# The multiply of the slot sums, on GpSimd instead of VectorE, in a graph kernel on one core

## The reference, cut to what matters

```python
h = x @ gcn_w                                      # one column
deg = segment_sum(ones, dst)                       # edges and loops
dis = rsqrt(deg)
msg = h[src] * (dis[src] * dis[dst])[:, None]
spa = sigmoid(segment_sum(msg, dst) + gcn_b)
return x * spa + x + chn_se                        # chn_se: the channel gate
```

## Time and profile before

| what | us |
|---|---|
| median of three runs | 8827.48 |
| lowest and highest run | 8819.26, 8833.81 |
| the profiled execution | 8835.66 |
| its span in the profile | 8833.9 |
| the loop, first one-hot (3441.20) to the first copy behind it (3668.73) | 227.5 |

### The profile page before, as it was taken

The page is one execution under the profiler, slowest core; times in us unless marked ns, Lnnn a source line. Parts: engine busy times, 40 slices in busy tenths (PEclk is TensorE's granted clock), DMA queues, the critical chain, the costliest instruction groups (busy, mean ns, idle before and its releaser), DMA issues. The chain is left out here.

```text
span 8833.9 us, 128810 instructions
## 1 busy us (share of the span) xinstructions
PE 5536.4 (63%) x23276; PEld 3811.3 (43%) x23277; DVE 4591.1 (52%) x13076; ACT 1797.8 (20%) x3217; POOL 4384.5 (50%) x4493
## 2 busy tenths in 40 slices
PE   5566666688888878976666666795444444444443
PEld 4333333455666556744444444453333333333332
DVE  8766666545555557854444444464333333333334
ACT  4000000046666631122222222341000000000000
POOL 0466666536666660034444444104666666666664
PEclk7566666699999987687877787896555555555555
DMA  2233333332222222322222222311111113111112
GB/s 78 58 100 105 102 105 103 94 113 82 82 84 80 83 66 62 128 87 65 65 65 63 67 67 64 75 32 44 53 52 44 44 44 43 43 43 43 44 43 60
DMA packets 310617, 612.39 MB, mean 69 GB/s; under 512 B 90042, under 2 KB 164102, under 8 KB 310344
## 3 DMA queue, kind: packets, MB, share of 16 engines
q0 software_dynamic: 185408, 469.86, 20.3%
q1 hardware_dynamic: 125064, 141.13, 5.3%
HBM read 566.94 MB, written 50.13 MB: 70 GB/s over the span
## 5 line engine op out<-in xcount | busy, mean ns | idle before, releaser
L834 PE MATMUL bank<-ring,oh 128*128 128x128 f32 x3552 | 1164.7, 475 | 1558.9 <-issue 838.8
L834 PEld LDWEIGHTS bank<-ring,oh 128*128 128x128 f32 x3552 | 861.8, 309 | 1861.8 <-issue 1150.4
L601 POOL DMA_INDIRECT ring<-q_table,stage_i x888 | 841.3, 947 | 1067.7 <-DVE ring L2181 693.9
L601 POOL DMA_INDIRECT ring<-h_table,stage_i x888 | 881.2, 992 | 641.9 <-issue 326.3
L1791 DVE TENSOR_TENSOR acc<-bank,acc 128x256 f32 x1776 | 753.6, 424 | 771.6 <-PE bank L907 386.3
L601 POOL DMA_INDIRECT ring<-fwd_table,stage_i x888 | 839.9, 946 | 578.1 <-issue 308.9
L601 POOL DMA_INDIRECT ring<-bwd_table,stage_i x888 | 840.1, 946 | 513.5 <-issue 272.8
L1826 DVE TENSOR_TENSOR acc<-bank,acc 128x128 f32 x1776 | 518.5, 292 | 1040.3 <-issue 689.2
L1252 ACT ACTIVATE ring<-big 128x889 f16<-128x889 f16 x840 | 832.4, 1033 | 514.4 <-PE bank L918 383.4
L918 PE MATMUL bank<-ring,big 128*128 128x445 f16 (+1 forms) x3360 | 819.0, 367 | 137.1 <-ACT ring L1252 108.5
L627 POOL DMA_INDIRECT big<-x_and_degree,stage_i x536 | 537.2, 1002 | 397.4 <-PE bank L867 225.9
(11 more groups left out here) (425 smaller groups left out, 7574.1 us busy)
## 6 DMA issues: line engine op xcount, KB each, us to landing
big<-places_in_block SPq DMA_DIRECT2D x111, 256.0 KB
acc<-places_in_block SPq DMA_DIRECT2D x74, 384.0 KB
ring<-h_table,stage_i POOLq DMA_INDIRECT x888
ring<-q_table,stage_i POOLq DMA_INDIRECT x888
ring<-fwd_table,stage_i POOLq DMA_INDIRECT x888
ring<-bwd_table,stage_i POOLq DMA_INDIRECT x888
big<-x_and_degree,stage_i POOLq DMA_INDIRECT x536
h_table<-hq SPq DMA_DIRECT2D x50, 128.0 KB, 1.7
```

The source lines that it names most:

```text
L601: pool.indirect_dma_start(out=gbuf[:, u % RING, 0:width], out_offset=None, in_=table, in_offset=bass.IndirectOffsetOnAxis(ap=stage_i[:, v, ...
L834: pe.matmul(bank[u % 4][:, 0:width], oh[:, u % 4, :], gbuf[:, u, 0:width], start=True, stop=True).then_inc(S["mm"], 1)
```

## The change

The 74 multiplies move from VectorE's queue to GpSimd's, ahead of its wait for `spa_in`, with the same operands and the same two waits. GpSimd runs them in order of the batches. VectorE's loop keeps the three one-hots of `select_slots`. A new semaphore, `slot_low`, is given by the low digits' one-hot, and PE waits for it in `slot_sums` beside `slot_prod`, because the two operands now come from two engines.

```diff
+            def place_values(b, k):        # in GpSimd's program
+                pool.wait_ge(S["slot_cp"], b + 1 + 3)
+                pool.wait_ge(S["slot_eq"], b + 1)
+                pool.tensor_tensor(high_val[k].rearrange("p u (s n r) -> p u s n r", s=3, r=2),
+                                   high_eq[k].rearrange("p u (n r) -> p u n r", r=2).unsqueeze(2).to_broadcast([P, BATCH, 3, NP // 2, 2]),
+                                   val_pairs[k].unsqueeze(3).to_broadcast([P, BATCH, 3, NP // 2, 2]), ALU.mult).then_inc(S["slot_prod"], 1)
+            for b in range(2):
+                place_values(b, b)
+            with pool.Fori(0, BATCHES // 3) as i:
+                for k in range(3):
+                    place_values(i * 3 + 2 + k, (2 + k) % 3)
...
             def slot_sums(b, k):
                 pe.wait_ge(S["slot_prod"], b + 1 + 3)
+                pe.wait_ge(S["slot_low"], b + 1)
...
-                dve.tensor_tensor(by_pairs(low_oh[k], P), iota_pairs(P), over(dst_lo[:, t, :], P), ALU.is_equal)
-
-            def place_values(b, k):
-                dve.wait_ge(S["slot_cp"], b + 1 + 3)
-                dve.wait_ge(S["slot_eq"], b + 1)
-                o = dve.tensor_tensor(...)
-                o.then_inc(S["slot_prod"], 1)
+                dve.tensor_tensor(by_pairs(low_oh[k], P), iota_pairs(P), over(dst_lo[:, t, :], P), ALU.is_equal).then_inc(S["slot_low"], 1)
...
                 select_slots(1, 1, 0)
-                place_values(0, 0)
                 with dve.Fori(0, BATCHES // 3) as i:
                     for k in range(3):
                         select_slots(i * 3 + 2 + k, (2 + k) % 3, i + (2 + k) // 3)
-                        place_values(i * 3 + 1 + k, (1 + k) % 3)
-                place_values(BATCHES - 1, 1)
```

More of the change, by code:

```diff
@@ L302, in build @@
         d_t d_at d_m d_h d_m2 d_h7 d_res x_in wb_in consts_in col_ready col_done gate_step
-        gate_done spa_in spa_out pass_ready p_split l2_oh l2_t l2_cp l2_p l2_add l2_silu
+        gate_done spa_in spa_out pass_ready slot_low p_split l2_oh l2_t l2_cp l2_p l2_add l2_silu
         l2_c l2_acc sqrt_in sqrt_out x2_done x2_mul x2_stat x2_agg x2_std x2_inv x2_out sp_waited p_diff p_high p_mid g_agg g_t1 g_a1 g_ab g_rz g_n
@@ L1750, in select_slots @@
                 dve.tensor_tensor(by_pairs(high_eq[k], NP), iota_pairs(NP), over(dst_hi[:, t, :], NP), ALU.is_equal).then_inc(S["slot_eq"], 1)
-                dve.tensor_tensor(by_pairs(low_oh[k], P), iota_pairs(P), over(dst_lo[:, t, :], P), ALU.is_equal)
-            def place_values(b, k):
-                dve.wait_ge(S["slot_cp"], b + 1 + 3)
-                dve.wait_ge(S["slot_eq"], b + 1)
-                o = dve.tensor_tensor(high_val[k].rearrange("p u (s n r) -> p u s n r", s=3, r=2),
-                                      by_pairs(high_eq[k], NP).unsqueeze(2).to_broadcast([P, BATCH, 3, NP // 2, 2]),
-                                      val_pairs[k].unsqueeze(3).to_broadcast([P, BATCH, 3, NP // 2, 2]), ALU.mult)
-                o.then_inc(S["slot_prod"], 1)
+                dve.tensor_tensor(by_pairs(low_oh[k], P), iota_pairs(P), over(dst_lo[:, t, :], P), ALU.is_equal).then_inc(S["slot_low"], 1)
             def node_sums(values, to):
```

## The result

The changed kernel took 8960.08 us (median of 4 runs, 8953.5 to 8963.07) against 8828.94 before: the ratio is 1.0143, with an interval of 1.0129 to 1.0156. That is 131 us slower, inside the range (8940 to 9090) and 60 us under the forecast of 9020.

A forecast was written before the change was run, and what follows sets the result against it. PE and VectorE were taken to bound the loop alike, 2.98 us a batch. One-hots 1.78 plus multiply 3.83 give 5.61; 74 x 5.61 - 1.78 = 413.4 us against 220.6, +193, so 9020 us, range 8940 to 9090.

The forecast's parts named there:

- The bound of the loop: In the loop: PE at 1.2 GHz and VectorE both full, 2.98 us per batch; relieving VectorE alone gives next to nothing.
- the two take turns: In the loop: VectorE's one-hots stand still while GpSimd multiplies, 1.78 + 3.83 us per batch; chance 0.65 at 3.39 to 4.28.
- L1917 beside L650: Trace row before the change: two-input VectorE instruction took its normal 0.68 us during a one-input GpSimd one, a counterexample to turns.
- the price of the multiply: One multiply of 1800 elements on GpSimd: 3.83 us, from 2.13 ns per element; ends 3.39 and 4.28.
- 5.61: Predicted us per batch of the loop: 1.78 for three one-hots on VectorE plus 3.83 for GpSimd's multiply.
- start-up hidden behind the other engine, 0.15: At hand-overs in the loop: 0.15 us of VectorE's start hides, about cancelled by GpSimd's 0.1 step to its next instruction.
- The forecast proper: Whole run with full turns in the loop, multiply at 3.39 to 4.28 us: 8987 to 9053 us, chance 0.65.
- The cover of PE and ACT: In the loop: three buffers hide PE's values and ACT's copy, about 2 us; without them up to 150 us more.
- Rival 2: Partial turns in the loop: GpSimd lets go early, by 0.46 us a batch or more; +159 to +127, about 8970; chance 0.12.
- Rival 1: No turns in the loop: instructions overlap, GpSimd's multiply alone sets the pace at 3.93 us; +70, 8898; chance 0.10.
- rival 3: Costlier multiply on GpSimd: 5.03 us, 6.81 per batch; +281, 9109; chance 0.10.
- rival 4: GpSimd multiplies in 1.68 us without turns; PE keeps 8827 (chance 0.02), or at 2.4 GHz 8746 (chance 0.01).

## Why the prediction was right, and where it was off

**The bound of the loop.** Right. PE at its lower clock was as long as VectorE; with the multiply left out from batch 2 on the whole run is at 1.0001 of before.

**GpSimd becomes the longest engine, and the two take turns.** Right, and shown from three sides: a one-hot taken out gives back its turn (58.6 us against 58), a multiply added costs a turn (3.0 us), and the two one-hots that no longer read both inputs from SBUF run beside the multiply. The Trainium skill's rule ("SBUF — State Buffer", "Who interferes with whom") held for every pair that the loop has, but for the tenths of a microsecond of start-up that hide at each hand-over. The place where the trace disagreed, L1917 beside L650, is real and was found again with other GpSimd instructions of one input.

**The term that was mis-sized** is the price of the multiply, "I take 3.83, the mean of the rows with two inputs". By itself it takes 3.21 us (3206 ns). That is 0.62 us of the 0.93 between 5.61 and 4.68. The mean was over two kinds of rows: two of the six (L644) had inputs one element apart, which is cheap, and float32 inputs 8 or more elements apart cost 2.2 ns per element at 1800 elements. The spread of the other four, 1761 to 2112 ns, is not explained by this. Neither kind is the loop's case, bf16 with one operand repeated; the lower end that I had given, 3.39, was nearest.

The other 0.31 us is what hides where one engine hands over to the other. The prediction let the "start-up hidden behind the other engine, 0.15" and GpSimd's step of 0.1 "about cancel"; they don't. How the 0.31 falls on the multiply and on the one-hots is a matter of counting: with 1.57 for the one-hots the multiply's turn is 3.1, by VectorE's queue in the kernel with the source one-hot ahead it is 1.78 and 2.95, and an extra multiply cost 3.0. Together 0.93 x 74 = 69 us, and 193 - 69 = 124, the loop's 126.

**Where luck helped.** The forecast proper, turns at 3.39 to 4.28 us, gave 8987 to 9053, and 8960 lies under it. It falls within 8940 to 9090 because of the room that had been left for partial turns, which don't happen.

**The cover of PE and ACT** held as predicted. GpSimd waited for ACT's copy here and there, some 20 us inside the loop, and with these waits moved away the loop stayed the same within 0.5 us, since VectorE used the time.

**The rivals.** Rival 2, partial turns, named 8970 and came nearest in time, but for a reason that the runs rule out: beyond the start-up no part of a multiply is open to the one-hots. A right number would have been no proof of it. Rival 1 fell with the timeline, rival 3 with the multiply's price by itself. What rival 4 says of PE, that at its clock it leaves nothing to gain, is shown by the kernel without the multiply; its fast multiply of 1.68 us is not what was measured.

## What to carry to other kernels

Before work is moved to an idle engine, ask what that engine shares with the one that is relieved: here each microsecond of two-input arithmetic on GpSimd was one in which VectorE's SBUF-to-SBUF instructions stood, so 1.09 us of VectorE's was traded for about 3 of both. And see first whether the relief can be worth anything: another engine was as long. In a profile such sharing shows as instructions of one engine that all end a fixed 0.3 or 0.4 us after one of the other, and as an engine that shows as busy all the time with less to do.

## What was unexpected of the hardware

- A two-input float32 multiply of 1800 elements on GpSimd takes 3.18 us with its inputs 1 or 4 elements apart, and 3.97 from 8 elements on (tried up to 2048). In bf16 it is 3.58 dense and 3.21 with the loop's repeated operands. That fewer bytes are fetched in the cheap cases would fit, but no run separates it.
- A GpSimd instruction's reported time holds its wait for VectorE: 3.21 us alone, 3.51 behind the 0.61 us one-hot, 3.85 behind the 0.95 us one.
- The same kernel before took 8829, 8989 and 7173 us on the chips of this study, while the changed kernel's loop took the same 353.5 us on the first and the last of these. Why the rest differs was not looked into.
